# Decoder with two mixture-of-experts layers: in the second experts ScalarE weights both row tiles directly behind the silu of the next expert

## What is computed

```python
logits = where(old_to_new == -1, -inf, x @ gate_weight.T)
top_v, top_i = top_k(softmax(logits), 8)           # weights are divided by their sum
# each token is put into a slot of each of its experts, up to CAP = 192 slots an expert
gu = einsum('ech,eoh->eco', xb, gate_up_proj)      # 192 rows x 512 -> 2 x 192
g, u = split(gu, 2)
h = silu(g) * u
out = einsum('eci,ehi->ech', h, down_proj)         # 192 rows x 192 -> 512
final = zeros.at[tok].add(out[slot] * weight)
```

## Time and profile before

| | |
|---|---|
| median of 3 runs | 2152.34 us (2149.24 to 2153.65) |
| the profiled execution | 2148.72 us, span 2147.0 us |
| busy, share of the span | TensorE 81%, VectorE 69%, ScalarE 45%, GpSimd 50% |
| granted TensorE clock, mean | 0.887 of full |
| the stage of the second experts | gate/up products from 1733.2 to 2091.8 us of the span |

### The profile page before, as it was taken

The page is one execution under the profiler, slowest core; times in us unless marked ns, Lnnn a source line. Parts: engine busy times, 40 slices in busy tenths (PEclk is TensorE's granted clock), DMA queues, the critical chain, the costliest instruction groups (busy, mean ns, idle before and its releaser), DMA issues. The chain is left out here.

```text
span 2147.0 us, 34548 instructions
## 1 busy us (share of the span) xinstructions
PE 1748.3 (81%) x9164; PEld 1395.6 (65%) x9165; DVE 1482.3 (69%) x2836; ACT 957.9 (45%) x1867; POOL 1083.6 (50%) x816
## 2 busy tenths in 40 slices
PE   4898989347999999999998898697851179999990
PEld 3566665236889888888887556464531178888880
DVE  4466867764777888887886323857679557777774
ACT  4354452312444444444443323535333157777773
POOL 1000715464667667667676000036357757777763
PEclk9898989666999999999999899887865589999995
DMA  8011011034888888888986623131010469999967
GB/s 325 27 40 59 20 59 40 1 102 141 209 212 212 206 220 225 219 219 216 232 228 134 224 39 59 44 74 59 1 59 1 170 179 256 258 248 258 256 150 255
DMA packets 138551, 318.72 MB, mean 148 GB/s; under 512 B 30840, under 2 KB 31320, under 8 KB 136824
## 3 DMA queue, kind: packets, MB, share of 16 engines
q1 hardware_dynamic: 71448, 201.68, 27.1%
q0 software_dynamic: 64752, 112.04, 26.9%
q10 hardware_dynamic: 2288, 4.29, 0.5%
HBM read 238.61 MB, written 97.62 MB: 157 GB/s over the span
## 5 line engine op out<-in xcount | busy, mean ns | idle before, releaser
L98 POOL DMA_INDIRECT tab_rows<-pair,slot x256 | 313.9, 1226 | 450.7 <-DVEq L752 299.3
L90 PE MATMUL gu<-wgu_h,xgT_h 128*128 x648 | 233.5, 360 | 7.2 <-DVE xgT_l L1428 3.6
L1253 POOL DMA_INDIRECT xg<-x_rows,ids x167 | 191.6, 1148 | 62.3 <-issue 48.5
L90 PE MATMUL gu<-wgu_l,xgT_h 128*128 x648 | 219.4, 339 | 0.0
L90 PE MATMUL gu<-wgu_h,xgT_l 128*128 x648 | 218.3, 337 | 0.0
L1308 ACT ACTIVATE ysb<-yp,wts 128x512 f32<-128x512 f32 x160 | 110.3, 689 | 144.6 <-PE yp L1535 144.6
L90 PE MATMUL guk<-xgT_hk,wgu_hk 128*128 128x192 f32 x576 | 161.2, 280 | 0.0
L90 PE MATMUL guk<-xgT_lk,wgu_hk 128*128 128x192 f32 x576 | 158.4, 275 | 0.0
L1298 ACT ACTIVATE sg<-gu 128x192 f32<-128x192 f32 x162 | 53.7, 331 | 234.4 <-PE gu L90 234.4
L90 PE MATMUL guk<-xgT_hk,wgu_lk 128*128 128x192 f32 x576 | 158.2, 275 | 0.0
L1428 DVE TENSOR_TENSOR xgT_l<-tpx,xgT_h 128x512 fp32r<-128x512 f32 x163 | 112.2, 688 | 54.4 <-ACT xgT_h L1294 52.2
(11 more groups left out here) (500 smaller groups left out, 5108.1 us busy)
## 6 DMA issues: line engine op xcount, KB each, us to landing
wgu_sb<-in_wgu SPq DMA_DIRECT2D x64, 768.0 KB
wgu_sbk<-in_wgu SPq DMA_DIRECT2D x48, 768.0 KB, 4.4
wd_sb<-in_wd SPq DMA_DIRECT2D x64, 256.0 KB
wd_sbk<-in_wd SPq DMA_DIRECT2D x48, 256.0 KB, 5.2
ct<-in_ctxT SPq DMA_DIRECT2D x8, 1024.0 KB, 4.9
wd_sb<-in_wd SPq DMA_DIRECT2D x64, 128.0 KB
wd_sbk<-in_wd SPq DMA_DIRECT2D x48, 128.0 KB, 5.8
odd_rows<-zero SPq DMA_DIRECT2D x1, 4352.0 KB, 15.5
```

Of the source, the lines that this page charges most:

```text
L90: i = nc.tensor.matmul(out, left(k), right(k), start=(start and k == 0 and m == 0), stop=(k == ops - 1 and m == 2))
L98: nc.gpsimd.indirect_dma_start(out=tab, out_offset=bass.IndirectOffsetOnAxis(ap=s["slot"][:, n:n + 1].bitcast(U32), axis=0), in_=s["pair"] ...
L1253: nc.gpsimd.indirect_dma_start(out=xg[:, t % G, :], out_offset=None, in_=x, in_offset=bass.IndirectOffsetOnAxis(ap=ids[:, t:t + 1].bitcast ...
```

## The change

In a step, ScalarE issues both `weighted` directly behind `silu` of the next expert, and `h_upper` and `rest_upper` follow. Before, the order was `silu`, `h_upper`, `weighted` of the even tile, `rest_upper`, `weighted` of the odd tile. Nothing else changes; the last step, which has no next expert, only weights its two tiles in both versions.

```diff
--- before.py
+++ after.py
@@ -1719,11 +1719,11 @@
                         down_upper(g + (n + 3) // NF, (n + 3) % NF, not first or n + 3 >= NF)
                     if not (last and n + 1 >= NF):
                         silu(g + (n + 1) // NF, (n + 1) % NF)
+                    weighted(g, 2 * n, not first or n >= G // 2)
+                    weighted(g, 2 * n + 1, not first or n >= G // 2)
+                    if not (last and n + 1 >= NF):
                         h_upper(g + (n + 1) // NF, (n + 1) % NF)
-                    weighted(g, 2 * n, not first or n >= G // 2)
-                    if not (last and n + 1 >= NF):
                         rest_upper(g + (n + 1) // NF, (n + 1) % NF)
-                    weighted(g, 2 * n + 1, not first or n >= G // 2)
 
             for n in range(2):
                 gate_up_upper(0, n, False)
```

## The result

Twenty executions of the changed kernel have a median of 2157.06 us (2125.06 to 2167.57), twenty of the kernel before 2151.28 (2145.60 to 2161.14). The stated ratio is 0.9929 [0.9909, 0.9949]. Sorted, the times are 2125.06, 2126.02, 2129.06, 2129.25, 2130.10, 2130.45, 2138.31, and then 2151.50 to 2167.57 for the other thirteen. So seven lie around 2129 (22 us, 1.0%, faster than before) and thirteen around 2158 (7 us, 0.3%, slower). By the ratio the change is 0.7% faster; by the medians of all twenty it is 0.3% slower. Nothing lies at the mean of the two.

What follows compares the result with a forecast made beforehand. A ring of ScalarE and VectorE, 7.66 us an expert, was the bound; cut below TensorE's 7.20, it gains 18.05, less 2.2 for gathers, plus 1.3 at the end: 17.1 us, from 2152.3 to 2135 us, range 2130 to 2147.

Steps and rivals of the forecast that it cites:

- The ring: ScalarE's casts and weightings plus VectorE's lower halves and product, second experts' stage: 7.66 us an expert, falling to 6.50.
- TensorE's 7.20: TensorE's floor per expert: 36 gate/up products, ten down products and eight transposes in 7.20 us, against 7.61 before.
- 2.2 for gathers: Allowance for heavier DMA load delaying gathers that TensorE needs: 0.05 us an expert over 44 experts, 2.2 us.
- The end: Last rounds: the last even scatter starts 8.57 in place of 9.91 us after the last gate/up, gaining 1.3 us.
- step 2: New ScalarE waits of the weightings for down products: cost nothing, h being whole 2.3 us before its down.
- Rival B: GpSimd's 0.94 us wait is its own, so its period stays 7.67 and only the end gains: 2151 us; chance 0.10.
- Rival C: Odd weighting's new wait on ScalarE delays h's casts, so TensorE waits before its down: slower, 2165 us; chance 0.06.
- step (4): DMA queues: weight load 0.6 us behind the odd gather, 7.13 us of work in 7.20; gather delays cost 2.2 us.
- Rival A: DMA engines become the bound, 7.43 us an expert, or gather landings of 8.5 us: gain 9.2, 2143 us; chance 0.22.
- growth of latency under load: Skill rule: HBM access up to 2 us under high load; gather landing would approach 8.4 us, period 7.40.
- step (3): GpSimd needs 7.03 us without its wait; scatters start earlier, odd gathers get 7.8 us of lead, nearly all in time.

Runs made afterwards that it cites:

- casts first: Changed kernel with the casts of h directly behind silu and both weightings last: 2152.56 us, ratio 1.0020.
- pairs with the old order: GpSimd issues both scatters, then both gathers 12 tiles ahead, with ScalarE's order as in the kernel before: 2149.12 us, ratio 1.0000.
- gathers further ahead: Changed kernel with gathers issued 12 tiles ahead of the scatter in place of 10: 2162.44 us, ratio 1.0029.
- light load: Changed kernel loading only a quarter of each gate/up weight load from the fifth expert on: 2127.36 us, ratio 0.9900.
- early load: Changed kernel with SyncE's gate/up load no longer waiting for the down tiles' lower halves: 2157.14 us, ratio 1.0052.
- first guards: Changed kernel, load waiting for a count GpSimd raises behind each odd scatter: 2167.07 us; the same with gathers 12 tiles ahead: 2166.99 us.
- guard that follows: Changed kernel, weight load waiting for a one-element GpSimd store behind each odd scatter: 2130.97 us, ratio 0.9915.
- more lead: The guard that follows, with gathers 12 tiles ahead in place of 10: 2146.93 us, ratio 0.9971.
- pairs: Changed kernel with GpSimd issuing both scatters of an expert, then the two gathers, 12 tiles ahead: 2147.39 us, ratio 0.9991.
- first guard: Changed kernel, SyncE's load waiting for a semaphore count that GpSimd raises behind each odd scatter: 2167.07 us, ratio 0.9949.

## Why the prediction was right and wrong

**Right.** The ring as the old bound (a period of 7.67 us in the casts first and in pairs with the old order, whatever GpSimd waits for), and TensorE's 7.20 as the new one. In the short execution 44 experts take 316.44 us, 18.4 less than 334.85, where the sum had 18.05 less 2.2 for gathers; no wait for gathers was left, so the 2.2 was nothing. The end gained too: the last even scatter starts at 2079.66, 19.77 us behind the last transposes in place of 21.26, 1.5 us against 1.3. A share of 0.97 at 270 GB/s was forecast as 0.98 and 270. ScalarE's wait for the odd down product before the casts of h (step 2) costs nothing: with a light load it stands there and TensorE has no gap. Rival B falls by its mechanism: GpSimd's 0.94 us goes in the casts first and the period stays. Rival C does not show in the changed kernel; its sign, TensorE waiting for h before its down, comes only with the gathers further ahead (24.1 us). The short group's middle, 2129, lies 6 us below the 2135 and 1 below the range: 2.2 of it are the gathers that did not wait, 2.2 that this execution was already ahead at the first transposes (1743.45 for 1745.60), 1.1 that the kernel before has its median of twenty at 2151.28, not 2152.34.

**Wrong: step (4), the queues.** It set the weight load against the odd *gather* ("0.6 behind it"; in the short execution it is 0.24 ahead, 1851.34 against 1851.58) and asked only what a gather's landing may grow to. (Its 6.4 us is that of gathers for which TensorE waited; by the lists of DMA issues from 1767 to 2043 the median gather lands in 5.6 us before, 5.4 in the short execution and 6.3 in the long one.) The scatter of odd rows, next to it in GpSimd's list, was not in the step, though it is the transfer on whose landing the next one waits. In the long execution its landing is 4.7 to 4.9 us while it starts 2.4 us ahead of the load, 6.4 and 7.0 at 0.18 us ahead, and 5.6 to 9.0 behind. Since its successor is then late as well, the chain keeps itself up for 24 periods. All 38 cost 38 x (7.93 - 7.20) = 27.7 us, nearly the 29 between the groups, and 23.0 of them lie in those 24. Rival A came nearest in kind (landings grow), but put the price on the share as such and at 7.43 us. The share of 0.97 belongs to the short group, and the long one has 0.92, so the mean load is not what tells them apart. The growth of latency under load that the prediction weighed does occur (odd scatters from 4.8 to 6.8 us, gathers from 5.6 to 6.3), and where a transfer starts against the load has a part in it; it is not the whole, for 1.7 us behind the load landings were 7.3 and 7.5 us early on and 5.9 to 6.2 later.

**Wrong: step (3), GpSimd.** Its 7.03 us without waits was read as "it follows". True, but it left 0.17 us of slack at 7.20, and with the scatter at 2.38 in place of 2.22 us nothing. And 0.75 of the 7.03 is the stretch of the odd scatter (2.22 in place of 1.47), which changes with the place of GpSimd's list against VectorE's block: on the even scatter it is 1.4 us and more, and the list alone takes 7.5. The step also has a lead of 5.8 us for a gather before the change; from its own numbers it is 14.4 - (6.2 - 2.2 + 5.75) = 4.65; the sum does not use it. The old kernel had 0.64 a period (0.94 - 0.30) to take up a late landing; the load there followed the scatter's end by 0.06 us too (1904.18 + 2.22 = 1906.40, load at 1906.46) and never changed places in the trace read. The change took the slack that kept the order.

**Left out: a wait in step (2).** ScalarE's weighting waits also for the scatter of the tile four before it, with the casts of h behind. The step priced only the wait for the down product. That other wait is 11.9 us in the changed kernel's long execution and 73.7 with the gathers further ahead.

**The number.** By the ratio the changed kernel's time is 0.9929 x 2151.28 = 2136.0 us, one from the forecast. That agreement is partly luck: of the 32 executions of it only four lie in 2130 to 2147. A range over a single centre could not hold this kernel; a rival "slower by a landing chain" at 7.9 us a period, with a chance near that of the forecast, would have.

**Shown and not.** Shown: that the ring set the old period, that the traffic is needed for the long group (light load), and, in the one long execution read, that most of its loss lies where GpSimd waits for odd landings. Supported, by few executions: that the order of load and odd scatter matters (early load and the first guards on one side, the guard that follows on the other). Not shown: that keeping the order is enough; with more lead the order was kept and ten of twelve executions lie between the groups. Read from one trace only: that a late even landing first turns the order. How often it does, and why pairs fall between the groups, stays open. A rival stands beside the chain: GpSimd's list full by itself, with a stretched even scatter, as in the end of the long execution and in the kernel with only the even weighting moved. No run moves it apart from the landings.

## What to carry to other kernels

When a change brings a stage down to one engine's floor, list the idle time left on *each* queue, and which transfers wait for the landing of their predecessor; a chain of such transfers beside a large load is a second bound that shows only once slack is gone. Count what a queue's own instructions take in each place that they may come to stand, not only where they stand now. Where two queues' order matters, pin it with a signal that truly follows the transfer, and look at the sorted times of many executions before trusting one profile.

## What the hardware showed that was not expected

- **A DMA instruction of GpSimd is stretched while VectorE runs the weight halves.** The odd scatter takes 1.47 or 2.38 us, the even one 1.57 or 2.96, a gather 0.98 or up to 2.63. VectorE's block is three subtractions in a row (L1750, L1754, L1755), with both inputs in SBUF; in the period shown the odd scatter ends at 1851.28, just as VectorE's L1755 does (1850.57 + 0.69 = 1851.26). The Trainium skill (SBUF — State Buffer, Who interferes with whom) says that a VectorE instruction with two SBUF inputs contends with a GpSimd instruction that reads SBUF, and that the lock on the shared ports is exclusive. The trace agrees so far that the scatter, begun during the block (1848.90), ends with it.
- **A semaphore count raised by GpSimd's list behind a DMA instruction takes effect before that DMA starts** (0.11 to 0.13 us before), while the one-element store behind it does not: the load then starts 1.6 us after the scatter, and GpSimd loses nothing.
- **Where a scatter starts against a load moves its landing.** An expert's load (768, 256 and 128 KB) starting 0.18 us behind a scatter rather than 2.4 went with 1.5 to 2.1 us more of landing, one that starts 0.46 ahead of it with 3.5, and one 1.7 ahead with 1.0 to 1.3 in the later part of the stage. The Trainium skill (DMA: Bandwidth & Descriptors, Queues, rings and completion order) has each DMA engine take whole packets from its rows in turn; that would make a transfer wait beside another's packets, but no run here shows it packet by packet.
- **The clock fell after short stalls.** In the long execution TensorE stood 2.20 us before 1908.82; the window from 1910 has a granted clock of 0.83, between the two levels of 1.2 and 2.4 GHz, and from the first gate/up product to the first down product it was 5.71 us (1909.67 to 1915.38) instead of 4.07 (1900.06 to 1904.13). The same after the stall of 2.76 us before 1966.84:

```profile
1910.00:1920.00 10.00, 10.00 (x67) 9.27 (x66) 6.20 (x13) 6.18 (x13) 6.92 (x7) 0.83 0.84 219
...
1970.00:1980.00 10.00, 10.00 (x75) 9.27 (x74) 6.40 (x12) 6.24 (x12) 8.00 (x6) 0.93 0.88 215
```

A chain that makes TensorE wait 2 us can so cost it 1.6 us more; twice in this stage, 3.3 of the 27.7 us. In the first guard, the longest kernel, five of the 35 windows from 1740 to 2090 show 0.83.
